# A four-layer transformer kernel: the last finish of the first token chain, and the norm behind the chain, moved into the work around them

## The reference, cut to what matters

```python
# layer 0, after its self attention: per token
x = x + cross_attention(layernorm(x), enc)
x = x + gelu(layernorm(x) @ mlp1_w + mlp1_b) @ mlp2_w + mlp2_b
# layer 1: per token
routed = softmax(x @ tok.T / 16) @ tok
ps_n, in_n = ln(x), ln(routed)
u, r = sigmoid([ps_n, in_n] @ W_u + b_u), sigmoid([ps_n, in_n] @ W_r + b_r)
cand = tanh([r * ps_n, in_n] @ W_n + b_n)
x = ln((1 - u) * x + u * cand) * g_out + beta_out
# layer 2: self attention, 16 heads of 64, over all 1024 tokens of a batch
h = layernorm(x)
x = softmax(q k.T / 8) v @ sa_wo + sa_bo + x
```

## Time and profile before

| what | value |
|---|---|
| median of three runs | 2271.69 us (2271.24 to 2276.19) |
| the profiled execution, its own time | 2273.37 us |
| its span in the profile | 2271.6 us |
| TensorE busy | 2058.4 us, 91% |
| VectorE, ScalarE, GpSimd busy | 1109.8, 948.3, 769.8 us |
| instructions | 27255 |

### The profile page before, as it was taken

One profiled execution on the slowest core, in us unless ns is written; L12 is line 12 of the kernel. 1 busy time (PEld: TensorE's weight loads), 2 busy tenths in 40 slices (PEclk: granted clock), 3 DMA queues, 4 the chain that ended last, 5 costly groups with the idle time before them and its releaser, 6 DMA issues. The chain is left out here.

```text
span 2271.6 us, 27255 instructions
## 1 busy us (share of the span) xinstructions
PE 2058.4 (91%) x10518; PEld 1232.6 (54%) x10558; DVE 1109.8 (49%) x2005; ACT 948.3 (42%) x1443; POOL 769.8 (34%) x510
## 2 busy tenths in 40 slices
PE   5889998798898949999999999999998989899997
PEld 3544444576676824444544454445444857676765
DVE  4666671625535266555555555554541153535353
ACT  4366666333433314555355535554553412222221
POOL 1212100122313125665566556565574010211111
PEclk9999999899998969999999999999999989999999
DMA  7724332000000040000000000000000500000000
GB/s 152 136 30 53 37 53 67 14 1 1 1 0 0 1 116 13 1 1 1 1 1 1 1 1 1 1 1 1 1 1 26 152 19 1 8 2 10 0 10 10
DMA packets 48202, 52.70 MB, mean 23 GB/s; under 512 B 14730, under 2 KB 38988, under 8 KB 47668
## 3 DMA queue, kind: packets, MB, share of 16 engines
q1 hardware_dynamic: 48084, 51.11, 10.8%
HBM read 41.24 MB, written 8.80 MB: 22 GB/s over the span
## 5 line engine op out<-in xcount | busy, mean ns | idle before, releaser
L1758 POOL TENSOR_TENSOR total<-total,pr 128x1024 f32<-128x1024 f32 x192 | 460.9, 2400 | 235.1 <-ACT pr L1899 216.6
L1899 ACT ACTIVATE pr<-sc 128x1024 f32<-128x1024 f32 x256 | 260.0, 1023 | 267.9 <-PE sc L1676 265.4
L1779 DVE TENSOR_REDUCE pmax<-ring 128x1 f32<-128x512 f32 x512 | 314.4, 684 | 98.2 <-PE ring L1638 98.2
L1676 PE MATMUL sc<-q_full,k_full 64*128 64x512 f32 x1024 | 294.8, 589 | 0.0
L1694 PE MATMUL o<-pr,v_pair 128*64 128x512 f32 x1024 | 247.7, 605 | 0.0
L1638 PE MATMUL ring<-k_round,q_round 64*128 64x512 f32 x512 | 213.7, 566 | 5.4 <-DVE k_round L1773 1.2
L629 ACT ACTIVATE probs<-s 128x512 f32<-128x512 f32 (+1 forms) x304 | 163.7, 575 | 105.7 <-PE s L342 59.1
L1029 POOL TENSOR_TENSOR c_scores<-c_scores,c_total 128x1024 f32<-128x1024 f32 (+1 forms) x48 | 77.0, 1616 | 316.9 <-DVE c_total L985 316.9
L1638 PEld LDWEIGHTS ring<-k_round,q_round 64*128 64x128 f32 x512 | 78.2, 189 | 137.2 <-DVE pmax L1779 115.9
L463 DVE TENSOR_REDUCE row_max<-s 128x1 f32<-128x640 f32 (+3 forms) x128 | 127.5, 1021 | 51.0 <-PE s L324 50.8
L1676 PEld LDWEIGHTS sc<-q_full,k_full 64*128 64x128 f32 x1024 | 128.9, 191 | 26.3 <-issue 17.1
(11 more groups left out here) (299 smaller groups left out, 3505.0 us busy)
## 6 DMA issues: line engine op xcount, KB each, us to landing
qk_dram<-qk_parts SPq DMA_DIRECT2D x32, 192.0 KB, 2.7
q_stack<-qk_dram SPq DMA_DIRECT2D x48, 128.0 KB
k_stack<-qk_dram SPq DMA_DIRECT2D x48, 128.0 KB
x<-in_x SPq DMA_DIRECT2D x4, 512.0 KB, 7.4
region<-in_L_xattn_mlp_w SPq DMA_DIRECT2D x2, 1024.0 KB, 7.2
region<-in_L_xattn_ff_w SPq DMA_DIRECT2D x1, 2048.0 KB, 19.2
...
```

Source lines behind the costliest of these rows:

```text
L1676: ins = te.matmul(s2[at % 2][:, j], kf[n % 2][head[j], keys], qf[n % 2][head[j], halves[half]], start=False, stop=True)
L1758: pool.tensor_tensor(out=total[half][:], in0=other[:], in1=probs[at % KEPT][:], op=ALU.add).then_inc(sums, 1)
L1779: dve.tensor_reduce(part_max[:, j, t, half:half + 1], ring[bank_of_max(i)][:], AX.X, ALU.max).then_inc(s1_free, 1)
L1899: act.activation(probs[here % KEPT][:], s2[at % 2][:], ACT.Exp).then_inc(s2_free, 1)
```

## The change

The chain's blocks 0 and 1 now take the tiles of batch 0, blocks 2 and 3 those of batch 1 (`own`), so both streams of a block are of one batch; all four blocks are written out. Batch 0 is thus finished in block 2. Its norm moves into the chain: statistics in block 2 (`moments7`), the reciprocal root behind block 2's n6 on GpSimd (`rstd7`), the normed tiles in block 3 (`normed7`), 16 transposes between block 3's down projections (`turn7`), 8 copies to `e.hT` (`kept7`).

The last block's mixing, its output norm and the norm of batch 1 move into the second attention: the mixing on GpSimd at the start; the output norm on VectorE at units 13 and 15 of pair 0 (`late`, `finish_chain`), with its reciprocal root on GpSimd ahead of the addition of unit 15; the norm of batch 1 in the same places of pair 1, kept in two unused slots of `aT`; its 16 transposes in pair 2, one group behind each value projection's end: one behind unit 13 and three behind unit 15 (`turn_late`, `keep_late`). `bias_out` goes to unit 13 of pair 3. SyncE asks for the second context's weights when the chain is finished, ahead of pair 2's shift, since they overwrite the mixed tiles. `part_norm2` is gone.

```diff
+        batch = lambda i: i // 2
+        own = lambda s, i: e.x[:, TB * batch(i) + 4 * (i % 2) + 2 * s:TB * batch(i) + 4 * (i % 2) + 2 * s + 2, :]
...
+        n7_bank = lambda q: ch.ps[q // 2][:, 1024 + 512 * (q % 2):1536 + 512 * (q % 2)]
...
+                def turn7(q):
+                    te.wait_ge(n7_h_made, q + 1)
+                    for c in range(KC):
+                        for t in range(2):
+                            ins = te.transpose(n7_bank(q)[:, (2 * c + t) * P:(2 * c + t + 1) * P],
+                                               n7_h(2 * q + t)[:, c * P:(c + 1) * P], e.ident[:])
+                    ins.then_inc(n7_turned, 1)
...
                             turn4(0)
+                        if last and t == 0:
+                            turn7(2 * s)
+                            turn7(2 * s + 1)
...
-            chain_blocks(te, emit)
+            for i in range(BLOCKS):
+                emit(i, i == 0, i == BLOCKS - 1)
...
+            def moments7():
+                for s in range(B):
+                    after(dve, tail.dve[s], "out.x", 1)
+                for t in range(TB):
+                    ins = dve.bn_stats(n7_stats[:, t, :], e.x[:, t, :])
+                ins.then_inc(n7_stats_made, 1)
+                dve.wait_ge(n7_stats_made, 1)
+                for t in range(TB):
+                    ins = dve.bn_aggr(n7_moments[:, t, :], n7_stats[:, t, :])
+                ins.then_inc(n7_moments_made, 1)
+
+            def normed7():
+                dve.wait_ge(n7_rstd_made, 1)
+                for t in range(TB):
+                    ins = dve.tensor_scalar(n7_h(t), e.x[:, t, :], n7_moments[:, t, 0:1], n7_rstd[:, t:t + 1],
+                                            ALU.subtract, ALU.mult)
+                    if t % 2:
+                        ins.then_inc(n7_h_made, 1)
 
...
                     norm_vector(dve, ch, "n3", i, x, lambda s: after_spare(dve, ch, s, "ca.x", i), streams=[s])
+                if last:
+                    normed7()
                 if not first:
...
+                if i == 2:
+                    moments7()
+
...
+                def kept7(q):
+                    act.wait_ge(n7_turned, q + 1)
+                    for c in range(KC):
+                        ins = act.activation(e.hT[:, c, q * 256:(q + 1) * 256], n7_bank(q)[:, c * 256:(c + 1) * 256],
+                                             ACT.Identity, bias=w.vec["l2_b"][:, c:c + 1], scale=w.vec["l2_g"][:, c:c + 1])
+                    ins.then_inc(n7_kept, 1)
...
+                if last:
+                    kept7(0)
+                    kept7(1)
                 turned4(0)
+                if last:
+                    kept7(2)
+                    kept7(3)
...
+                if i == 2:
+                    rstd7()
                 for name in ("n4", "n5"):
                     norm_gpsimd(pool, ch, e, name, i)
-                if not last:
-                    norm_gpsimd(pool, ch, e, "n2", i + 1)
-
+
+                if last:
...
+        vec, LATE, TURNS_LATE = e.w0.vec, 2, 4
+        last_x = lambda s: e.x[:, TILES - 4 + 2 * s:TILES - 2 + 2 * s, :]
+        late_h = aT[:, 3:5, :].rearrange("p a (t c) -> p (a t) c", c=C)
+        late_bank = lambda q: ring[q % 2]
...
-            for n, (tile, src) in enumerate(context2_loads(A, e.ctx_w0, 0)):
-                sp.dma_start(tile, src).then_inc(e.ctx_w0_in[min(n, 1)], 16)
             sp.wait_ge(shift_set, 2)
             for n in range(PAIRS):
+                if n == LATE:
+                    sp.wait_ge(finished, 2)
+                    for i, (tile, src) in enumerate(context2_loads(A, e.ctx_w0, 0)):
+                        sp.dma_start(tile, src).then_inc(e.ctx_w0_in[min(i, 1)], 16)
...
+            def turn_late(q):
+                te.wait_ge(late_h_made, 1)
+                if q == 0:
+                    te.wait_ge(top_made, 5 * (LATE + 1) + 1)
+                elif q == 1:
+                    te.wait_ge(kept, 6 * (LATE + 1) + 5)
+                else:
+                    te.wait_ge(late_kept, q - 1)
+                for c in range(KC):
+                    for t in range(2):
+                        ins = te.transpose(late_bank(q)[:, (2 * c + t) * P:(2 * c + t + 1) * P],
+                                           late_h[:, 2 * q + t, c * P:(c + 1) * P], e.ident[:])
+                ins.then_inc(late_turned, 1)
 
             def project_out(group, t):
...
                             project(n + 1, 4 + VALUES_AT.index(u + 1))
+                    if n == LATE and u + 1 in VALUES_AT:
+                        for q in (range(1) if u + 1 == VALUES_AT[0] else range(1, TURNS_LATE)):
+                            turn_late(q)
...
+            pool.wait_ge(power_set, 1)
+            for s in two:
+                pool.tensor_tensor(out=e.cand0[s][:], in0=e.cand0[s][:], in1=e.xc0[s][:], op=ALU.subtract
+                                   ).then_inc(cand_less, 1)
+            for s in two:
+                pool.wait_ge(cand_less, s + 1)
+                pool.tensor_tensor(out=e.cand0[s][:], in0=e.cand0[s][:], in1=e.u0[s][:], op=ALU.mult
+                                   ).then_inc(cand_gated, 1)
+            for s in two:
+                pool.wait_ge(cand_gated, s + 1)
+                pool.tensor_tensor(out=e.xc0[s][:], in0=e.xc0[s][:], in1=e.cand0[s][:], op=ALU.add).then_inc(mixed, 1)
+
+            def rstd_of(count, moments, rstd, moments_made, shifted, made):
+                pool.wait_ge(moments_made, 1)
+                pool.tensor_tensor(out=rstd[:], in0=moments[:, :, 1], in1=e.eps[:].to_broadcast([P, count]),
+                                   op=ALU.add).then_inc(shifted, 1)
+                pool.wait_ge(shifted, 1)
+                pool.tensor_tensor(out=rstd[:], in0=rstd[:], in1=power[:, 0:count], op=ALU.pow).then_inc(made, 1)
+
             for n in range(PAIRS):
                 for u in range(U):
...
+                        rstd_of(4, n6_moments, n6_rstd, n6_moments_made, n6_shifted, n6_rstd_made)
+                    if n == 1 and u == 15:
+                        rstd_of(TB, n7_moments, n7_rstd, n7_moments_made, n7_shifted, n7_rstd_made)
                     if kt == 0:
...
                 dve.wait_ge(raw_made, 2 * n + h + 1)
+                if n == 3 and h == 0:
+                    dve.wait_ge(late_turned, TURNS_LATE)
...
             def bias_out():
                 dve.wait_ge(wo_in, 32)
+                dve.wait_ge(late_h_made, 1)
...
+            def finish_chain():
+                dve.wait_ge(n6_rstd_made, 1)
+                for s in two:
+                    for t in two:
+                        ins = dve.scalar_tensor_tensor(
+                            out=last_x(s)[:, t, :], in0=e.xc0[s][:, t, :], scalar=n6_moments[:, 2 * s + t, 0:1],
+                            in1=vec["o_g"][:], op0=ALU.subtract, op1=ALU.mult)
+                    ins.then_inc(n6_h_made, 1)
+                for s in two:
+                    dve.wait_ge(n6_h_made, s + 1)
+                    for t in two:
+                        ins = dve.scalar_tensor_tensor(
+                            out=last_x(s)[:, t, :], in0=last_x(s)[:, t, :], scalar=n6_rstd[:, 2 * s + t:2 * s + t + 1],
+                            in1=vec["o_b"][:], op0=ALU.mult, op1=ALU.add)
+                    ins.then_inc(finished, 1)
+
+            def late(n, u):
+
+                if (n, u) == (0, 13):
+                    dve.wait_ge(mixed, 2)
+                    moments_of(4, lambda t: e.xc0[t // 2][:, t % 2, :], n6_stats, n6_moments, n6_stats_made,
+                               n6_moments_made)
+                elif (n, u) == (0, 15):
+                    finish_chain()
+                elif (n, u) == (1, 13):
+                    dve.wait_ge(finished, 2)
+                    moments_of(TB, lambda t: e.x[:, TB + t, :], n7_stats, n7_moments, n7_stats_made, n7_moments_made)
+                elif (n, u) == (1, 15):
+                    dve.wait_ge(n7_rstd_made, 1)
+                    for t in range(TB):
+                        ins = dve.tensor_scalar(late_h[:, t, :], e.x[:, TB + t, :], n7_moments[:, t, 0:1],
+                                                n7_rstd[:, t:t + 1], ALU.subtract, ALU.mult)
+                    ins.then_inc(late_h_made, 1)
+                elif (n, u) == (3, 13):
+                    bias_out()
 
...
-            bias_out()
...
+            def keep_late(q):
+                act.wait_ge(late_turned, q + 1)
+                for c in range(KC):
+                    ins = act.activation(e.hT[:, c, T + q * 256:T + (q + 1) * 256], late_bank(q)[:, c * 256:(c + 1) * 256],
+                                         ACT.Identity, bias=vec["l2_b"][:, c:c + 1], scale=vec["l2_g"][:, c:c + 1])
+                ins.then_inc(late_kept, 1)
...
+        e.u0, e.cand0 = ([first[:, c0 + 512 * s:c0 + 512 * s + 512].rearrange("p (t c) -> p t c", c=C) for s in range(B)]
+                         for c0 in (T, 3 * T))
```

(1 more changed line is left out.)

146 lines of the change are left out of this document (68 added, 78 removed).

## The result

| what | before | after |
|---|---|---|
| median of the runs | 2272.45 us (2271.24 to 2276.19, 4 runs) | 2250.20 us (2250.11 to 2250.31, 4 runs) |
| ratio after to before | | 0.990, 95% interval 0.9887 to 0.9912 |
| the profiled execution, its span | 2273.37, 2271.6 us | 2250.27, 2248.3 us |

The change gains 22.25 us by the medians, 23.3 by the spans of the profiled executions. The forecast was 2248.8, its range 2243.5 to 2254.5.

A forecast was written before the change was run, and what follows sets the result against it. The attention was taken as bound by TensorE, with a nearly idle 32.00 us stage ahead of it to win. Terms -29.5 + 0.6 + 2.7 + 1.5 + 1.8 = -22.9 from 2271.69 gave 2248.8 us, range 2243.5 to 2254.5.

The forecast's parts named there:

- Handover: Chain's end to attention's first projection: start at 798.1 instead of 827.57, 16 added transposes costing 1.7 included; -29.5 us.
- the 0.81: Difference between chain block steps of 96.78 and 97.59 us, taken as granted-clock noise; writing out the loop would win nothing.
- What else goes into the chain: Batch 0's statistics, power, normed tiles and keepings in chain blocks 2 and 3 fit in idle time: cost 0.
- Start of the attention: GpSimd's mixing delays VectorE's last rounding of q and k, which lets the maxima start: +0.6 us (0 to 1.24).
- Turns of the second batch: Pair 2: 16 transposes cost 1.7 us on full TensorE, plus a bank-wait stall of 0.8 to 1.0; +2.7 us.
- the 1.7 of my lower bound: Pair 2's 16 transposes with no stall for a bank: 1.7 us; the upper bound, with two stalls, was 3.7.
- Finish and norm in pairs 0 and 1: VectorE's strings may delay GpSimd's last addition, stalling TensorE 2.2 us in each pair; a third taken, +1.5 (0 to 4.4).
- The output bias: Pair 3: VectorE's 4.41 us bias holds back GpSimd's last two additions, stalling TensorE 1.9; +1.8 us (0 to 4.4).
- The cover holds: Rival: VectorE and GpSimd find gaps, neither finish nor bias reaches TensorE; -26.5, 2245.2 us, chance 0.22.
- GpSimd's additions become the bound: Rival: at the late steps every VectorE string goes first and the bias stalls TensorE 2.5; 2253.0 us, chance 0.17.
- The attention loses its clock: Rival: new stalls ending pairs 0 to 3 halve the clock; dips 2254 to 2259 us, 0.06; slower than before, 0.02.
- The handover is not won: Rival: something else, weights or code, holds the first projection; with half the gap left 2264 us, chance 0.03.

The follow-up runs named there:

- the ten made from it: Nine edited versions of the kernel after the change, plus that kernel unedited once more; medians from 2245.45 to 2254.03 us.
- the written-out kernel: Kernel before the change with only the chain's loop over the middle blocks written out as four blocks: 2273.26 us against 2273.74, ratio 0.9998.
- the three edits together: Kernel after, with the bias in halves, transposes spread over pairs 2 and 3, and mixing behind the last rounding: 2246.77 us against 2250.20.
- the second execution: Kernel after the change, run once more with nothing changed: median 2250.17 us, against 2250.20 the first time.

## Why the prediction was right, and where not

- **Handover, -29.5.** Measured -28.9. The gap's end behind the tanh (0.31 for 0.29) and the transposes (1.8 for 1.7) were right. The other 0.5 stood ahead of the chain's last block: 0.23 of it when the chain began (400.66, before 400.43), the rest by the first sum of its first block (437.68, before 437.20). That stretch of 37.0 alone took from 36.45 to 37.33 in the kernel after and the ten made from it, so the 0.5 is scatter and no cost of the change. It isn't the 0.81 that I had put down to the clock's placing and kept as noise. That one is no noise: the written-out kernel has the same steps from tanh to tanh (97.55, 96.82, 97.56), and why the middle one is shorter stays open.
- **What else goes into the chain, 0.** Right: the sum behind the down projection still waits 11.78 for TensorE, and what the last block lost is the transposes.
- **Start of the attention, +0.6** (0 to 1.24). Measured +0.71 to 0.72, by the mechanism named; one wait on GpSimd's side takes it away. From the first projection to pair 0 it doesn't show (36.51 against 36.54): the values projection that follows took 4.91 instead of 5.84, since the granted clock rose earlier in it (its mean over the projection is 0.75, before 0.62). That offset was luck: it took 6.52 in the second execution, at a mean of 0.55.
- **Turns of the second batch, +2.7.** Measured 2.76, with the wait for the bank of 0.82 where 0.8 to 1.0 was forecast. Where they are spread over two pairs and no other wait hides them, in the three edits together, the 1.7 of my lower bound comes out as 0.87 and 0.88.
- **Finish and norm in pairs 0 and 1, +1.5** (0 to 4.4). **This step failed: measured 0.** The time hides it, since other terms were off the other way. I had the slack and the power's length right (1.02 and 1.65 for 4 and 8 columns), but left the order of arrival at "a third". The start times show why it is nothing: VectorE's string waits for the power, and the addition stands right behind the power on GpSimd itself, so that GpSimd starts it at 936.07 and VectorE its string at 936.13. The addition is in hand when the string arrives, and it is the string that waits (6.84 for 2.67), in idle time of 14.31. With the order turned round pair 1 cost 2.32. The bound was right, the choice inside it was not.
- **The output bias, +1.8.** Measured 2.14, of which 1.91 are the wait. Right in mechanism (a reduction in its place: 0; half the length: 0, the slack of 2.39 not used up). One detail was wrong: the bias doesn't wait for an addition to end. The split's last small operation runs in a gap between two additions, and the bias follows it in the same gap, so that GpSimd loses the full 4.34. It holds back the last three additions (one record stands from 1036.86 to 1043.66), not the last two.
- **The sum.** -28.9 + 2.76 + 2.14 + 0.7 behind the attention is -23.3 on the spans, and -22.25 by the medians; forecast -22.9. On the spans, the misses are +0.6 (handover), -0.6 (start, where the clock gave the rounding's 0.7 back), -1.5 (pairs 0 and 1), +0.4 (pairs 2 and 3) and +0.7 (behind the attention, which I had at 0). They come to -0.4: the total is nearer than its terms deserve. The +0.7 is no cost found: from the last pair to the end the kernel after and the ten made from it took 631.06 to 633.26, and before 631.98. By the time, 2250.20 for 2248.8 is inside the range, and part of the difference is that the median before is 2272.45 with its fourth run, not 2271.69.
- **The rivals.** *The cover holds* was half true: the finish never reached TensorE, the bias did. *GpSimd's additions become the bound* is true of the bias alone. *The attention loses its clock* is out: 1.00 over all pairs, with waits of 0.82 and 1.91. *The handover is not won* is out.
